# Mixture-of-experts gates sent through DRAM: one copy and two half-partition spreads per pair, or eight copies and one full-partition spread per expert

## The reference

```python
x = x + conv(_ln_c(x))          # windowed attention, 8x8 windows, 4 heads
t = _to_tokens(x)               # 4 x 16384 tokens of 64 channels
router_probs = softmax(_ln_t(t) @ router_w + router_b)        # 8 experts
top_p, top_i = top_k(router_probs, 2)
top_p = top_p / sum(top_p)
expert_out = einsum('bnd,edc->bnec', _ln_t(t), expert_w) + expert_b
t = t + einsum('bnk,bnkc->bnc', top_p, take_along_axis(expert_out, top_i))
```

## Time and profile before

| what | value |
|---|---|
| time, median of 3 executions | 1091.67 us (1088.63 to 1094.42) |
| time of the profiled execution | 1087.85 us |
| span of the profiled execution | 1086.1 us |
| PE busy | 1014.9 us, 93% |
| DVE, ACT, POOL busy | 827.3, 797.9, 432.7 us |
| DMA: bytes moved, share of the 16 engines | 189.60 MB; 72.5% by SP's queue |

### The profile page before, as it was taken

How to read it: one execution, slowest core, us unless ns; L and a number is a source line. 1 busy time by engine, 2 the same in 40 slices (tenths; PEclk the granted TensorE clock), 3 DMA queues, 4 the chain that set the end, 5 groups by cost and what they waited for, 6 DMA issues and landing times.

```text
span 1086.1 us, 39091 instructions
## 1 busy us (share of the span) xinstructions
PE 1014.9 (93%) x16762; PEld 576.0 (53%) x16762; DVE 827.3 (76%) x1355; ACT 797.9 (73%) x1280; POOL 432.7 (40%) x509
## 2 busy tenths in 40 slices
PE   4898899999999999999999999999999999989867
PEld 3455555555555555556555555555555555555312
DVE  4456987877787787777787887777878877787775
ACT  1498888878787877878878888877888877667510
POOL 1002434334443443444434434444344346434550
PEclk9999999999999999999999999999999999999988
DMA  6003678987777898777787987777788876876885
GB/s 200 1 22 72 158 177 190 216 194 175 184 180 169 190 214 190 183 193 181 188 190 184 215 214 180 179 176 185 186 190 215 214 185 160 194 155 145 207 194 138
DMA packets 48872, 189.60 MB, mean 175 GB/s; under 512 B 10494, under 2 KB 10750, under 8 KB 32572
## 3 DMA queue, kind: packets, MB, share of 16 engines
q1 hardware_dynamic: 48700, 187.10, 72.5%
HBM read 151.15 MB, written 18.87 MB: 157 GB/s over the span
## 4 chain that ended last, share of the span: by engine, by line
PE 82%; DVE 6%; ACT 4%; issue 4%; POOL 1%; DMA 1%; SPq 0%; DVEq 0%; ACTq 0%; POOLq 0%
PE bank L711 19%; PE bank L590 12%; PE bank L607 11%; PE bank L624 7%; PE bank L564 5%; PE bank L534 5%; PE bank L631 5%; PE bank L574 4%; PE bank L643 3%; PE bank L652 2%; PE bank L662 2%; PE bank L511 2%; DVE gz L1870 2%; PE bank L525 1%; ACT lg L1279 1%
## 5 line engine op out<-in xcount | busy, mean ns | idle before, releaser
L711 PE MATMUL bank<-gz,wex 64*64 64x512 f32 x2048 | 254.0, 606 | 6.4 <-DVE ob L1919 4.8
L1848 DVE TENSOR_REDUCE mx<-bank 128x16 f32<-128x1024 f32 x128 | 156.1, 1220 | 112.2 <-PE bank L590 111.9
L1657 POOL TENSOR_TENSOR gz<-gz,tt 128x1024 f32<-128x1024 f32 x94 | 226.7, 2426 | 29.7 <-DMA gz<-gates_dram 29.7
L1870 DVE TENSOR_TENSOR gz<-gz,tt 128x1024 f32<-128x1024 f32 x156 | 202.2, 1314 | 1.1 <-DMA gz<-gates_dram 1.1
L1855 DVE TENSOR_TENSOR probs<-bank,mx 128x1024 f32<-128x1024 f32 x128 | 156.6, 1223 | 43.9 <-PE bank L607 40.8
L1618 POOL TENSOR_TENSOR tt<-prj,xs 128x512 f32<-128x512 f32 x64 | 82.7, 1316 | 250.8 <-ACT prj L1268 250.8
L607 PE MATMUL bank<-cst,probs 128*128 128x128 f32 x1024 | 166.6, 285 | 3.9 <-issue 2.1
L1251 ACT ACTIVATE pt<-bank 128x512 f32<-128x512 f32 x256 | 151.0, 590 | 24.7 <-PE bank L607 22.7
L607 PEld LDWEIGHTS bank<-cst,probs 128*128 128x128 f32 x1024 | 108.0, 140 | 100.1 <-issue 63.1
L590 PE MATMUL bank<-km,qs 32*64 32x128 f32 x4096 | 144.2, 276 | 4.1 <-issue 2.6
L590 PEld LDWEIGHTS bank<-km,qs 32*64 32x64 f32 x4096 | 112.4, 133 | 63.1 <-issue 62.4
(11 more groups left out here) (123 smaller groups left out, 1394.9 us busy)
## 6 DMA issues: line engine op xcount, KB each, us to landing
gz<-gates_dram SPq DMA_DIRECT2D x250, 512.0 KB, 7.9
xs<-in_x SPq DMA_DIRECT2D x32, 512.0 KB, 10.1
tx<-tt SPq DMA_DIRECT2D x128, 128.0 KB, 6.4
out<-ob SPq DMA_DIRECT2D x128, 128.0 KB, 6.0
gz<-in_rel SPq DMA_DIRECT2D x1, 2048.0 KB, 8.0
gates_dram<-gt_rs SPq DMA_DIRECT2D x32, 64.0 KB
cst<-in_consts SPq DMA_DIRECT2D x1, 359.0 KB, 2.9
tt<-in_weights SPq DMA_DIRECT2D x4, 64.0 KB, 3.8
```

What stands on the lines that cost most here:

```text
L711: last = mm(bank[64 * x:64 * x + 64, Y_BANK + a, :], wex[64 * a:64 * a + 64, e, :], gz[64 * a:64 * a + 64, s.pair(e)[1], e % 2, x * CH:(x ...
L1657: tt_(gz[:, k, e % 2, :], gz[:, k, e % 2, :], tt[s.buf(4)][:, :], op=ALU.mult).then_inc(z_pool, 1)
L1848: red(mx[g % 2][:, :], two_banks(S_BANK).rearrange("p (c k) -> p c k", k=N), axis=AX_X, op=ALU.max).then_inc(max_done, 1)
L1870: tt_(gz[:, k, e % 2, :], gz[:, k, e % 2, :], tt[s.buf(4)][:, :], op=ALU.mult).then_inc(z_dve, 1)
```

## The change

The rows of a gate go to DRAM in eight copies for each image, and each expert's gates come back in one transfer to all 128 partitions.

- `gates_dram` grows from 16 rows of 1,024 tokens per strip to 8 experts by 16 rows: for each expert eight copies of image 0's row and eight of image 1's.
- `write_gates` issues two DMAs instead of one, one for each half of the strip. Each reads 16 partitions, every one eight times, and writes 128 rows of 2 KB: 256 KB each, 512 KB for a strip where there were 64 KB. Both count on `gates_written`, so the counts waited for double.
- `spread_gates` still issues two DMAs of 512 KB for a pair. Each now serves one expert and all 128 partitions with 4 KB on each; eight neighbouring partitions read the same copy.
- The columns of part 3 are put in the order expert, image (they were image, expert), by a rearranged access in the last copy of `place_gates`, on POOL and on DVE, and `late_gates` picks its selection matrices accordingly. No instruction is added by that.

On PE, DVE, ACT and POOL the instructions and their order are the same as before. Only SP's stream differs. The core of the diff:

```diff
-        gates_dram = nc.dram_tensor("gates_dram", [4, 2 * E, LT], F32, kind="Internal").ap()
+        COPIES = 8
+        gates_dram = nc.dram_tensor("gates_dram", [4, E, 2 * COPIES, LT], F32, kind="Internal").ap()
...
                 sp.wait_ge(gsb_ready, s.count(2, 1))
-                sp.dma_start(gates_dram[s.buf(4)].rearrange("m (x t) -> x m t", x=2), gt_rs[s.buf(2)][96:P, :]
-                             ).then_inc(gates_written, 16)
+                rows = gates_dram[s.buf(4)].rearrange("e (a r) t -> (e a) r t", a=2)
+                for x in range(2):
+                    sp.dma_start(rows[:, :, x * CH:(x + 1) * CH],
+                                 gt_rs[s.buf(2)][96 + 16 * x:112 + 16 * x, :].unsqueeze(1).broadcast_to(
+                                     [2 * E, COPIES, CH])).then_inc(gates_written, 16)
...
-                    sp.wait_ge(gates_written, s.count(16, 16))
+                    sp.wait_ge(gates_written, s.count(32, 32))
...
-                for a in range(2):
-                    sp.dma_start(gz[64 * a:64 * a + 64, k, :, :].rearrange("p e t -> p (e t)"),
-                                 gates_dram[s.buf(4), E * a + 2 * q:E * a + 2 * q + 2, :].rearrange(
-                                     "e t -> (e t)").partition_broadcast(64)).then_inc(gz_loaded[k], 16)
+                for e2 in range(2):
+                    sp.dma_start(gz[:, k, e2, :], gates_dram[s.buf(4), 2 * q + e2].unsqueeze(1).broadcast_to(
+                        [2 * COPIES, P // (2 * COPIES), LT])).then_inc(gz_loaded[k], 16)
...
-                nc.gpsimd.tensor_copy(part(3).bitcast(F32), tiles(gsum)).then_inc(gp_ready, 1)
+                nc.gpsimd.tensor_copy(by_expert(part(3).bitcast(F32)), tiles4(gsum)).then_inc(gp_ready, 1)
```

More of the change, by code:

```diff
@@ L696, in late_gates @@
                     for a in range(2):
-                        last = mm(bank[64 * a:64 * a + 64, b + x, :], late_select[x][:, a, e, :],
+                        last = mm(bank[64 * a:64 * a + 64, b + x, :], late_select[x][:, (2 * e + a) // E, (2 * e + a) % E, :],
                                   gt_rs[s.buf(2)][late_rows[x], :], start=True, stop=True)
@@ L1299, in move_scaled_gates @@
                 act.wait_ge(gt_full, s.count(1, 1))
-                wait(act, gates_written, s.count(16, 16, lag=2))
+                wait(act, gates_written, s.count(32, 32, lag=2))
                 af(gt_rs[s.buf(2)][96:P, :], bank[96:P, PRE, :], ACT.Copy).then_inc(gsb_ready, 1)
@@ L1625, in place_gates @@
                 part = lambda k: gp[:, :, k, :, :]
+                tiles4 = lambda t: t[:, :, :].rearrange("p (x t a) e -> p t x e a", x=2, a=2)
+                by_expert = lambda t: t.rearrange("p t x (e a) -> p t x e a", a=2)
                 pool.wait_ge(g_ready, s.count(2, 2))
@@ L1899, in place_gates @@
                 dve.wait_ge(gp_ready, s.count(4, 3))
-                nc.vector.tensor_copy(part(3).bitcast(F32), tiles(gsum)).then_inc(gp_ready, 1)
+                nc.vector.tensor_copy(by_expert(part(3).bitcast(F32)), tiles4(gsum)).then_inc(gp_ready, 1)
             def token_statistics(s):
```

## The result

The changed kernel takes 1104.59 us (median of 4 runs, 1099.49 to 1115.43), the kernel before, beside it on the same chip, 1093.05 us (4 runs, 1088.63 to 1097.65): a ratio of 1.0117 [1.0074, 1.016], 1.2% slower. The profiled execution took 1101.16 us with a span of 1099.3, against 1087.85 and 1086.1 before: +13.2 us of span. The forecast was 1092 us, no change, with a range of 1085 to 1100.

The account below looks back on a forecast made before the run. PE was taken as the limit in the loop, so only start-up, drain or a full DMA queue could matter. +1.5 at start-up, 0 in the loop and -0.75 in the drain gave +0.75 us: 1092 us, range 1085 to 1100.

Parts of the forecast that it names:

- The steady part: Loop, period 30.47 us: slack of 6.3 us at POOL and 5.3 us on SP hides the later write; cost 0.
- The ring wait on SP: Loop: SP waits for PE to free the ring before the next spread, so 5.3 us of earlier delay vanish there.
- The spread's gain: Each pair of 1.05 MB moves at 344 instead of 223 GB/s, 3.05 us for 4.70: 1.65 us gained (0 to 1.65).
- rival B: New spreads still move 223 GB/s; sum +4.05 us, 1095.7 us by the median, loop DMA share near 0.90; chance 0.32.
- The write: Gates to DRAM: issue to first spread becomes 0.69 + 2.5 + 3.2 = 6.4 us, +3.0 us (+1.35 to +4.0).
- Start-up: First strip: first pair lands at 108.84 instead of 107.49, DVE follows POOL and ends later; +1.5 us (-0.3 to +2.5).
- Drain: Last strip: last spread lands at 1076.0, DVE's product ends before POOL's, PE ends at 1079.4; -0.75 us (+0.2 to -2.1).
- The sum: Whole kernel: +1.5 at start-up and -0.75 in the drain give +0.75 us, said as 1092 us, no measurable change.
- C: Slower: the write saturates the DMA queue in the loop, share 1.0; +24 us, 1116 us by the median; chance 0.11.
- Rival D: Faster: the drain's gates come early, freeing DVE's `es` and `gsum` from POOL's products; -6.5 us, 1085 us; chance 0.14.
- The signs: New profile: loop pair landing from 7.7 towards 6 us, DMA share 0.68 and PE busy above 243 us, 250 to 500 us.
- I am wrong if the period of the loop moves: Loop: the forecast fails if the period moves from 30.47 us, or if the drain shortens by more than 2 us.

Follow-up runs that it names:

- e5: The kernel before with its 64 KB write issued, waited for, issued again and waited for, so each first spread leaves some 3.3 us later; ratio 1.0372 to before.
- e4: The kernel before with 448 KB more written per strip behind the fourth spread, to a scratch tensor nobody reads; ratio 1.004 to before.
- e3: The kernel before with its 64 KB write, each expert's gates spread from one row to all 128 partitions by one transfer; ratio 0.9829 to before.
- e10: The kernel before with one row spread to all 128 partitions, read as 16 outer steps of 8 repetitions; ratio 0.9869 to before.
- e9: The kernel before with the loop's token swaps issued ahead of each strip's first spread, nothing else; ratio 0.9959 to before.
- e13: The changed kernel with swaps ahead of the first spread, first and last strip sent the old way, sixteen copies instead of eight; ratio 1.066 to before.

## Why the prediction was wrong

**The steady part** is the step that failed: "Anything below about 5 us per strip is therefore hidden." The ring wait on SP did take up the delay, as the step said (from 43 such waits to 24). But that wait was also what kept SP's transfers apart. Without it they leave in one row, and what meets the fuller queue isn't a consumer of gates but PE's instruction loads. Cost in after: 6.2 us, of which 5.8 are such pauses; in e5, without the gain of the new spread, 37.2. The added bytes do the same on a smaller scale (e4, 7.4). How much of the 6.2 would be left if the spread had gained what was forecast stays open, since no run has the 512 KB write with a spread of e3's rate.

Two numbers on the table had spoken against the step. The period of 30.47 us was taken from one pair of strips; the same copy on POOL gives 778.3 / 25 = 31.13 us as a mean, so the kernel before already lost 0.66 us a strip to something. And the 4% "issue" in the chain were passed over. The slack was weighed against those who wait on a semaphore, and a load of instructions shows no semaphore.

**The spread's gain** was mis-sized: 1.65 us a pair, measured 1.05 MB at 241 GB/s, 4.36 us against 4.70: 0.35 us. The row of 344 GB/s was chosen because it is of 128-partition transfers; what decides is how the transfer is cut into steps (e3 against e10). That was rival B, and its doubt was the right one. The share of the loop, 0.85, lies nearer to B's 0.90 than to 0.68.

**The write** was right as a total: 6.4 us from issue to first spread forecast, 6.44 measured; the 1.6 us more that were thought possible did not come. Its parts were not: SP's two issues alone took 2.64 us, where 0.69 and 0.64 were assumed. So the total agrees in part by luck.

**Start-up**: +1.5 us forecast, +3.1 measured until strip 2. For the first pair the measured terms give 3.08 - 0.35 = 2.73 us; POOL's first product is 14.07 us behind the write's issue, before 11.40, which is 2.67. The terms of the landing were right but for the spread. The path behind it was another. DVE in the kernel after, and its `var` in the kernel before:

```profile
110.34 1.23 DVE L1875 TENSOR_TENSOR gz<-gz,tt 128x1024 f32<-128x1024 f32 x1 [1.11 <-DMA gz<-gates_dram]
...
111.79 2.14 DVE L1831 TENSOR_SCALAR var<-var 128x256 f32<-128x256 f32 x1
```

```profile
111.17 0.28 DVE L1826 TENSOR_SCALAR var<-var 128x256 f32<-128x256 f32 x1
```

DVE did not come after POOL: both products start when the pair has landed, and DVE's ends at 111.57, only 0.6 us later than before. It is the short `var` behind it that takes 2.14 us in place of 0.28, while POOL's product runs until 113.78.

**Drain**: -0.75 us forecast, +3.9 measured after strip 27. From the last write to POOL's last product it is 17.71 us against 14.27, +3.4. SP needed 4.73 and 3.68 us to issue the swaps and the store behind the write, so the last spread left 9.81 us after it (before 5.81); the gain of 0.35 hardly helps. The step let only the landing move, and took SP's issues as they were.

**The sum**: +0.75 against +13.2. Of the 12.5 us between them 6.2 are the loop, 4.7 the drain and 1.6 the start-up. Rival B's +4.05 had the spread right, and none of the rivals had the loop by this cause; C had a loss in the loop, but by a full queue, which needs 1.0 and saw 0.85. Rival D, a gain in the drain, isn't borne out: POOL's products there still start with 37.7 us of waits.

**The signs** that I named: the landing (8.7 us, not towards 6) and the share spoke for B, as said. PE's busy time stayed above the 243 us that I had set (243.12), and the loop was slower all the same: the bound was too coarse, as it allowed 1.3 us in 250, 0.5%, where the whole loss of the loop is 0.8%. "I am wrong if the period of the loop moves" was the test that caught it: 31.38 us as a mean, before 31.13.

## What to carry to other kernels

Before a delay is booked as hidden by slack on an issuing queue, ask what that slack was doing: if it spaced the transfers, its loss shows on whoever shares the DMA engines. For an engine with very many small instructions, read "issue" in the chain and the waits, compare the mean period of all strips with one clean one, and look for the instruction loads in the pauses. A wait for a write is better filled with other issues (e9: two lines, -0.4%) than made worthwhile by a faster transfer behind it; and the cut of a transfer, its outermost steps, is to be tried before its rate is put in a sum.

## What the runs showed of the hardware

- PE's program is brought in while it runs, 133 loads of 16 KB and 256 instructions, through the same DMA engines as the data. When they are late PE stands still, for up to 3.1 us (e5), with no releaser in the trace. Behind five such pauses the granted clock of e5 fell to the 1.2 GHz level, for 20.4 us in all. What sets when a load is asked for isn't in the trace; and whether the depth of the queue counts, or the moment at which its fullest part meets PE's small matmuls, these runs don't separate: e4 has a share of 82.1% and 12.1 us of pauses, e5 76.1% and 28.3.
- A broadcast to 128 partitions moves 369 GB/s in 128 steps and 241 GB/s in 16 steps of 8; 32 steps of 4 land as fast as 128.
- A large write in pieces of 2 KB slows the issues behind it on the same queue: in the last strip four swaps took SP 2.44 us behind the 64 KB write of the kernel before, and 4.73 us behind the 512 KB of the kernel after; behind the 1 MB of e13 it was 6 to 10 us.
